# B's low half by accumulating transfers, the first output's low products behind the sixth convolution, and the fifth convolution by three products, in a convolution and gated low-rank product kernel

## What is computed

```python
def cond(x, c, weight, c_weight, bias):
    out = conv_general_dilated(x, weight, padding=[(4, 4)], feature_group_count=4)
    return out + einsum('nd,od->no', c, c_weight)[:, :, None] + bias[None, :, None]

def ffn(h, A_w, B_w, Wq_w, keys):        # A_w (512, 1024), B_w (1024, 512), Wq_w (16, 1024), keys (64, 16)
    scores = einsum('bsr,er->bse', einsum('bsd,rd->bsr', h, Wq_w), keys)
    top_vals, top_idx = top_k(scores, 16)
    gate = sum(one_hot(top_idx, 64) * softmax(top_vals)[..., None], axis=-2)
    z = einsum('bsd,nd->bsn', h, A_w)     # 512 values, 8 for each of the 64 experts
    return einsum('bsn,on->bso', z * gate per expert, B_w) * 2.0

x = x + ffn(cond(x, ...), ...)
```

## Time and profile before

| what | value |
|---|---|
| median of 3 runs | 234.52 us (233.66 to 234.68) |
| the profiled execution's own time | 234.13 us |
| its span in the profile | 232.3 us |
| TensorE busy with matmuls | 228.0 us, 98% |
| VectorE busy | 193.3 us, 83% |
| ScalarE busy | 99.3 us, 43% |
| mean DMA rate over the span | 167 GB/s |

### The profile page before, as it was taken

The page is one execution under the profiler, slowest core; times in us unless marked ns, Lnnn a source line. Parts: engine busy times, 40 slices in busy tenths (PEclk is TensorE's granted clock), DMA queues, the critical chain, the costliest instruction groups (busy, mean ns, idle before and its releaser), DMA issues.

```text
span 232.3 us, 4018 instructions
## 1 busy us (share of the span) xinstructions
PE 228.0 (98%) x1383; PEld 203.5 (88%) x1383; DVE 193.3 (83%) x466; ACT 99.3 (43%) x246; POOL 1.5 (1%) x10
## 2 busy tenths in 40 slices
PE   7999999999999999999999999999999999999995
PEld 7998998898989889898898989889898989898884
DVE  1799899999969899998999899898998979847232
ACT  4997768246262353525334352532535242101100
POOL 2000000000000000000000000000000000000000
PEclk9999999999999999999999999999999999999999
DMA  6999064742734528164362826347272343553632
GB/s 207 374 402 393 20 198 123 268 138 93 234 128 113 208 80 279 53 188 158 92 246 70 264 76 187 139 100 257 65 251 91 67 162 93 183 144 131 190 125 92
DMA packets 23781, 38.79 MB, mean 167 GB/s; under 512 B 2768, under 2 KB 11856, under 8 KB 23760
## 3 DMA queue, kind: packets, MB, share of 16 engines
q1 hardware_dynamic: 23616, 38.45, 50.0%
q10 hardware_dynamic: 144, 0.08, 0.1%
HBM read 25.94 MB, written 12.58 MB: 166 GB/s over the span
## 4 chain that ended last, share of the span: by engine, by line
PE 90%; ACT 5%; DMA 2%; SPq 1%; issue 1%; DVE 0%; ACTq 0%
PE p_z L646 35%; PE p_out L684 13%; PE p_out L685 13%; PE p_out L692 13%; PE p_conv L600 10%; ACT h_c L395 3%; PE p_out L646 3%; PE p_conv L543 3%; DMA x_blk<-in_x_blocks 2%; ACT a_hi L359 1%; ACT x_hi L359 1%; PE p_z L668 1%; ACT h_hi L359 0%; SPq L279 0%; PE p_t L658 0%
## 5 line engine op out<-in xcount | busy, mean ns | idle before, releaser
L684 PE MATMUL p_out<-b_hi,zt_hi 128*128 128x512 f32 (+1 forms) x128 | 50.1, 392 | 0.0
L685 PE MATMUL p_out<-b_hi,zt_lo 128*128 128x512 f32 (+1 forms) x128 | 50.0, 392 | 0.0
L692 PE MATMUL p_out<-b_lo,zt_hi 128*128 128x512 f32 (+1 forms) x128 | 34.4, 391 | 0.0
L646 PE MATMUL p_z<-a_hi,h_lo 128*128 128x264 f32 x240 | 34.2, 285 | 0.0
L646 PE MATMUL p_z<-a_hi,h_hi 128*128 128x264 f32 x240 | 34.1, 285 | 0.0
L646 PE MATMUL p_z<-a_lo,h_hi 128*128 128x264 f32 x240 | 34.0, 284 | 0.0
L646 PEld LDWEIGHTS p_z<-a_hi,h_hi 128*128 128x128 f32 x240 | 32.0, 188 | 1.6 <-issue 0.4
L646 PEld LDWEIGHTS p_z<-a_hi,h_lo 128*128 128x128 f32 x240 | 31.2, 188 | 0.0
L646 PEld LDWEIGHTS p_z<-a_lo,h_hi 128*128 128x128 f32 x240 | 31.0, 188 | 0.0
L685 PEld LDWEIGHTS p_out<-b_hi,zt_lo 128*128 128x128 f32 x128 | 24.0, 188 | 5.6
L684 PEld LDWEIGHTS p_out<-b_hi,zt_hi 128*128 128x128 f32 x128 | 24.0, 188 | 5.6
(11 more groups left out here) (105 smaller groups left out, 266.6 us busy)
## 6 DMA issues: line engine op xcount, KB each, us to landing
x_nat<-in_x_rows SPq DMA_DIRECT2D x16, 512.0 KB, 4.9
out_dram<-x_nat SPq DMA_DIRECT2D x31, 256.0 KB, 3.1
x_blk<-in_x_blocks SPq DMA_DIRECT2D x14, 516.0 KB, 3.9
z_dram<-a_raw SPq DMA_DIRECT2D x64, 64.0 KB, 1.8
a_raw<-z_dram SPq DMA_DIRECT2D x16, 256.0 KB, 3.3
a_raw<-in_a_wq SPq DMA_DIRECT2D x8, 264.0 KB, 6.4
x_nat<-in_b_w SPq DMA_DIRECT2D x4, 512.0 KB, 9.5
x_blk<-in_x_blocks SPq DMA_DIRECT2D x2, 258.0 KB, 3.6
```

Source lines behind the costliest of these rows:

```text
L646: mm = nc.tensor.matmul(z_bank(t, b)[:, 0:HB], h[:, t % 2, r, :], a[:, r, b * HB:(b + 1) * HB], start=k == 0 and r == 0, stop=k == 2 and r ...
L684: nc.tensor.matmul(dst, zt_hi[:, t % 2, c, :], b_hi[:, c, cols], start=c == 0, stop=False)
L685: nc.tensor.matmul(dst, zt_lo[:, t % 2, c, :], b_hi[:, c, cols], start=False, stop=False)
L692: mm = nc.tensor.matmul(dst, zt_hi[:, t % 2, c, :], b_lo[:, c, start:stop], start=False, stop=c == JC - 1)
```

## The change

The constant TW goes from 5 to 4, so that tile 4 is convolved by `conv_sum` and `conv_pair` with the differences, the shared weights of group 1 (`sum_w(1)`, `split_ws(1)`) and `add_shared`. VectorE no longer computes b_lo. Instead ScalarE writes -b_hi into b_lo (`negate_b`: a copy of b_raw scaled by -1 and rounded), and GpSimd's queue issues for each piece a transfer from b_raw to b_lo that adds to what lies there. s_blo becomes one semaphore for each piece. The orders of TensorE, ScalarE and VectorE are rewritten: `out_low(0, 0)` and `out_low(0, 1)` stand behind `conv_pair(5)`, ahead of the output of tile 1; `add(0, 0)` stands behind `copy_scores(3)` and `add(0, 1)` behind `take_first(3)`; on VectorE `split_z(0)` stands behind `top_first(2)`.

```diff
--- before.py
+++ after.py
@@ -15,7 +15,7 @@
 
 
 NT = 16
-TW = 5
+TW = 4
 TS = 5
 NN = 8
 NG = 4
@@ -162,7 +162,8 @@
         s_ahi = sem("s_ahi")
         s_alo = sem("s_alo")
         s_bhi = sem("s_bhi")
-        s_blo = sem("s_blo")
+        s_blo = [sem(f"s_blo{c}") for c in range(JC)]
+        s_bneg = sem("s_bneg")
         s_cw = sem("s_cw")
         s_up = sem("s_up")
         s_u = sem("s_u")
@@ -266,7 +267,7 @@
                 if t >= XN:
                     sp.wait_ge(s_st[t % XN], 32 * (t // XN))
                 else:
-                    sp.wait_ge(s_blo, t + 1)
+                    sp.wait_ge(s_blo[t], 16)
                 sp.dma_start(x_nat[:, t % XN, :], x_rows[t]).then_inc(s_xn[t % XN], 16)
 
             def store(t, k):
@@ -353,6 +354,10 @@
             nc.gpsimd.tensor_copy(cw[:, 2:NG], sm[:, SMALL_CW + 2 * CI:SMALL_CW + NG * CI].rearrange("d (g c) -> d g c", c=CI)
                                   .unsqueeze(2).to_broadcast([P, NG - 2, R, CI])).then_inc(s_cw, 1)
 
+            for c in range(JC):
+                pool.wait_ge(s_bneg, c + 1)
+                pool.dma_start(b_lo[:, c, :].bitcast(F32), b_raw[:, c, :], accum_op=ALU.add).then_inc(s_blo[c], 16)
+
         @block.scalar
         def _(act):
             def high(dst, src, s):
@@ -422,6 +427,9 @@
             def split_b(c):
                 act.wait_ge(s_b[c], 16)
                 high(b_hi[:, c, :], b_raw[:, c, :], s_bhi)
+
+            def negate_b(c):
+                nc.scalar.activation(b_lo[:, c, :], b_raw[:, c, :], ACT.Copy, scale=-1.0).then_inc(s_bneg, 1)
 
             def split_z(t):
                 if t >= 2:
@@ -482,27 +490,31 @@
             add_u(3)
             exp(0)
             split_h(2)
-            split_x(4)
-            split_keys()
+            split_b(0)
+            negate_b(0)
+            split_b(1)
             take_q(1)
             split_w(1)
             copy_q(1)
-            split_b(0)
-            split_b(1)
+            split_x(4)
+            sum_w(1)
             take_q(2)
+            negate_b(1)
             exp(1)
             copy_q(2)
-            split_h(3)
-            split_z(0)
             split_b(2)
             split_b(3)
-            add_u(4)
+            split_z(0)
+            negate_b(2)
+            negate_b(3)
             exp(2)
-            sum_w(1)
+            split_h(3)
+            add_u_shared(4)
             split_x(5)
             take_q(3)
             split_z(1)
             split_h(4)
+            split_keys()
             for i in range(3, NT):
                 if i > 3 and i != NT - 2:
                     take_q(i)
@@ -688,7 +700,7 @@
                 dst, start, stop = parts(t)[k]
                 for c in range(JC):
                     if t == 0 and k == 0:
-                        pe.wait_ge(s_blo, c + 1)
+                        pe.wait_ge(s_blo[c], 16)
                     mm = nc.tensor.matmul(dst, zt_hi[:, t % 2, c, :], b_lo[:, c, start:stop], start=False, stop=c == JC - 1)
                 mm.then_inc(s_out, 1)
 
@@ -722,11 +734,10 @@
             z_product(2, 1, (0,), range(R // 2, R))
             z_product(2, 2, (0,), range(R))
             scores(2)
-            conv(4)
+            conv_sum(4)
+            conv_pair(4)
             out_high(0, 0)
             out_high(0, 1)
-            out_low(0, 0)
-            out_low(0, 1)
             for i in range(3, NT):
                 for k in range(3):
                     z_product(i, k, (1,), range(R))
@@ -740,6 +751,9 @@
                 scores(i)
                 if i + 2 < NT:
                     conv_pair(i + 2)
+                if i == 3:
+                    out_low(0, 0)
+                    out_low(0, 1)
 
 
                 if i >= NT - 2:
@@ -817,10 +831,6 @@
             def round_a(r):
                 dve.wait_ge(s_a[r], 16)
                 nc.vector.tensor_copy(a_hi[:, r, :], a_raw[:, r, :]).then_inc(s_ahd, 1)
-
-            def split_b(c):
-                dve.wait_ge(s_bhi, c + 1)
-                low(b_lo[:, c, :], b_raw[:, c, :], b_hi[:, c, :], s_blo)
 
             def split_z(t):
                 dve.wait_ge(s_zthi, t + 1)
@@ -959,55 +969,58 @@
             gate(0)
             turn_z(0)
             split_h(2)
-            split_x(4)
+            differ(4, 0)
+            differ(4, 1)
             turn_h(3, 0)
             turn_h(3, 1)
+            sum_w(1)
             split_w(1)
             copy_scores(1)
             top_first(1)
-            split_b(0)
+            split_x(4)
             take_first(1)
             top_second(1)
-            split_b(1)
+            split_ws(1)
             take_second(1)
             weigh(1)
             invert(1)
             gate(1)
             turn_z(1)
-            split_z(0)
-            split_h(3)
             copy_scores(2)
             top_first(2)
-            split_b(2)
+            split_z(0)
             take_first(2)
             top_second(2)
-            split_b(3)
             take_second(2)
             weigh(2)
             invert(2)
             gate(2)
-            sum_w(1)
+            split_h(3)
+            turn_z(2)
             differ(5, 0)
             differ(5, 1)
-            split_ws(1)
-            turn_z(2)
+            add_shared(4, 0)
+            add_shared(4, 1)
             turn_h(4, 0)
             turn_h(4, 1)
             split_x(5)
             split_z(1)
             split_h(4)
-            add(0, 0)
             for i in range(3, NT):
                 if i + 3 < NT:
                     differ(i + 3, 0)
                 copy_scores(i)
+                if i == 3:
+                    add(0, 0)
                 top_first(i)
                 if i + 3 < NT:
                     differ(i + 3, 1)
                 take_first(i)
+                if i == 3:
+                    add(0, 1)
                 if 3 < i < NT - 3:
                     split_z(i - 1)
-                if i < NT - 3:
+                if 3 < i < NT - 3:
                     add(i - 3, 1)
                 top_second(i)
                 take_second(i)
```

## The result

The changed kernel took 237.3 us at the median of 8 runs (235.52 to 241.74), the kernel before 234.5 (233.66 to 234.94). The ratio is 1.0091, with a 95% interval of 1.0066 to 1.0117: slower, by 2.1 us. This ratio and all that follow leave out executions that lie over 1.5% above the fastest of the same kernel: here those of 240.1 and 241.74 us, and in the experiments, among others, three of about 278.7 us with a mean granted clock of 0.757 (held_behind_z_out, all_moved) and one of 374.5 us with 0.566 (vector_subtracts). 234.5 was forecast, with a range to 235.7. The times of the changed kernel are also spread over several us, where those of before lie within 1.3.

The account below looks back on a forecast made before the run. TensorE's stream was taken as the bound (busy 228.0 of 232.3 us). Terms +0.03 - 0.15 + 0.08 = -0.04 took the profiled 234.13 to 234.09; with the median 0.39 higher, the forecast was 234.5, range 233.5 to 235.7.

Parts of the forecast that it names:

- B's low half: Step pricing negate_b and the four adding transfers into b_lo: cost 0 if a single transfer takes 4.5 to 9.5 us.
- the 4.5 to 6 us: Time assumed for each adding transfer of b_lo, since the DMA engines were taken as mostly free then.
- The slow rival: Adding transfers limit throughput, piece 3 holds out_low(0, 0); at 6.5 us each +2.1 us, 236.6; chance 0.10.
- The rival that POOL's issuing holds VectorE: Holds of 1 us for pieces 0 and 1 in the chain to split_z(0) give +1.9 us, 236.4; chance 0.08.
- TensorE's work: conv_sum(4) in place of conv(4): 12 products fall to 9, taking 0.70 us out of TensorE's stream.
- the walk to split_z(0): VectorE's order up to split_z(0), ending at 38.60: the saved 0.70 us becomes a 0.73 us wait, +0.03.
- After that: From out_high(0, 0) through z_product(3) to conv_sum(5): the 0.15 us gap at gate(2) goes, -0.15; added VectorE work costs TensorE nothing.
- the low products' new place: out_low(0, *) behind conv_pair(5): out_high(1, 0) waits for add(0, 0) until 52.72 instead of 52.64, +0.08 us.
- the +0.03: Start of out_high(0, 0) at 38.74 instead of 38.71, a loss of 0.03 us.
- the sum of -0.04: Total over the walked steps in us: +0.03 - 0.15 + 0.08.
- The chance: Probability 0.14 that the change is slower by over 0.5%, against 0.82 for same and 0.04 for faster.

Follow-up runs that it names:

- held_behind_z_out: Changed kernel with POOL waiting for z_out(1) to land before issuing piece 1, so pieces 1 to 3 go later; ratio 1.0066 to the kernel before.
- all_moved: Changed kernel with load_rows(0), z_out(2) with z_in(2), split_z(0) and copy_q(3) moved, adding transfers kept; ratio 1.0045 to the kernel before, 1.0032 when repeated.
- vector_subtracts: Changed kernel without transfers and negate_b; VectorE computes b_lo, split_z(0) moved forward, row loads moved back; ratio 1.0123 to the kernel before.
- changed_again: The changed kernel run once more without edit, the source of the second profile (execution of 237.74 us); ratio 1.0112 to the kernel before.
- rows_later: Changed kernel with only load_rows(0) moved behind z_in(1) on SP's queue; ratio 1.0041 to the kernel before.
- no_transfers: Changed kernel with the four adding transfers left out, their waiters waiting for negate_b instead; ratio 1.0008 to the kernel before.
- early_z_split: Changed kernel without the transfers and with split_z(0) moved forward on ScalarE and VectorE; ratio 0.9986 to the kernel before.
- the first profile: The first profile taken of the changed kernel, without further edit, from an execution of 240.1 us.

## Why the prediction was wrong

- **The step that failed** is "B's low half", and in it the sentence that between 4.5 and 9.5 us of a single transfer the cost is 0. The bounds held, though not the 4.5 to 6 us that was taken within them: the four took 5.6, 7.4, 6.3 and 7.8 us in changed_again, and the DMA engines were not mostly free. Wrong was to price them by their own deadlines alone. Their cost is in what they do to others' landings: the last part of `z_out(1)` from 1.8 to 6.4 and 8.2 us, z_in(1) from 2.5 to 6.9 in rows_later. SP's queue was followed for whether `z_out(1)` is issued in time, not for when it lands.
- **The wait that was left out.** `turn_z(2)` waits for `z_out(1)` to land (the `s_zo` wait of `turn_z`). In the kernel before it had some 5 us to spare (z_in(1) is issued on the landing at 40.78, `turn_z(2)` starts at 45.84), so no row names it; the walk brought `turn_z(2)` forward to 42.2, 1.4 us behind the landing, and I did not list it among what the DMA engines' load could reach. It is the wait that took 3.72 us of VectorE's time.
- **The slow rival** was built on the right worry, adding transfers as a limit of throughput, at the wrong place: piece 3, issued at 40.1 in changed_again, was there by 48, before `out_low(0, 0)` wanted it. The rival that POOL's issuing holds VectorE did not occur (2.09 us with and without it, above).
- **TensorE's work and the walk to split_z(0)** were right: nine products and a start of `out_high(0, 0)` 2.86 us after `conv_sum(4)`, walked as 2.88; the gain of 0.70 us eaten by that wait (no_transfers 1.0008, early_z_split 0.9986).
- **After that and the low products' new place** were right within 0.15 us, by no_transfers. One slip of sign is in it: the +0.03 was counted as time gained, so that `conv_pair(5)` was walked to 50.77 instead of 50.80 (52.79 + 0.03 - 1.87 - 0.15); the sum of -0.04 does not use it.
- **The chance** of 0.14 for slower rested on prices of waits one by one. The four transfers add 2.1 MB to the 4.2 MB that the kernel before moves from 28 to 52 us, and took 39.2% of the DMA engines' time from 28 to 56 us in changed_again, where all other transfers, 3.99 MB, took 47.0%. The bytes were known beforehand, and they alone should have moved more chance to slower.

## What to carry to other kernels

A transfer is priced twice: by who waits for it, and by which small transfers on a tight round trip it meets on the same DMA engines. List every wait on a DMA in its window, with its slack, even those that the trace of before doesn't show because they were never late. And where a saving comes out of a stream that is always busy, look for the next value it needs: here the place of one value's split in the engines' orders held back what three matmuls had saved (0.5 of the 0.70 us came back with it).

## What the runs showed of the hardware that was not expected

- Adding transfers from SBUF to SBUF kept the DMA engines fully busy at about 215 GB/s (42 to 46 us of the first profile, the last of `z_out(1)` among them). They took twice the engines' time that plain copies of the same bytes took (39.2% against 19.0% of 28 us). POOL mostly needs 0.86 to 1.0 us to issue one and 0.53 to 0.67 for a plain copy.
- POOL's subtraction of 128x1024 took 2.4 to 3.4 us, and VectorE's instructions with two SBUF inputs that ran into it got longer: 3.3 us instead of 1.2.
- After 3.6 us without matmuls TensorE ran at the granted level of 1.2 GHz for over 3 us; after the 1.97 us of the second profile the granted clock stayed at 1.00.
